# Loading the second phase's weights in two halves, with the turned queries and keys in between

## The reference

```
x = x + self_attention(layernorm(x))     # 16 heads of 128, q and k rms-normed, softmax, wo
x = x + cross_attention(layernorm(x), ctx)  # 16 heads of 32, causal mask; Wq, Wkv_expand, Wout
x = x + ffn(layernorm(x))                # 512 -> 1408 -> 512 (Wg, Wu, Wd), with 8 low-rank
                                         # experts (Ag Bg Au Bu Ad Bd), the top 2 of 8 by router Wr
```

## Time and profile before

| | |
|---|---|
| median of 3 runs | 2593.97 us (2593.64 to 2600.76) |
| the profiled execution, its own time | 2594.01 us |
| its span | 2592.2 us |
| mean granted clock of TensorE | 0.981 of full speed |
| TensorE busy | 2473.8 us |
| DVE, ACT, POOL busy | 1558.7, 1337.1, 870.1 us |
| first phase | from the start to about 1260 us |

### The profile page before, as it was taken

The page is one execution under the profiler, slowest core; times in us unless marked ns, Lnnn a source line. Parts: engine busy times, 40 slices in busy tenths (PEclk is TensorE's granted clock), DMA queues, the critical chain, the costliest instruction groups (busy, mean ns, idle before and its releaser), DMA issues.

```text
span 2592.2 us, 47471 instructions
## 1 busy us (share of the span) xinstructions
PE 2473.8 (95%) x16414; PEld 1335.5 (52%) x16414; DVE 1558.7 (60%) x3578; ACT 1337.1 (52%) x4095; POOL 870.1 (34%) x801
## 2 busy tenths in 40 slices
PE   6999999999999999999889999999999999999988
PEld 3544455554554555445454464464464464465466
DVE  6777756666666666667456655555655645645634
ACT  4555555555555555555445554454454454554433
POOL 2333333333333333333123323323323323423412
PEclk9999999999999999999969999999999999999999
DMA  5677677876786767796511001001001001000000
GB/s 155 149 179 173 142 158 153 180 164 155 156 175 143 171 144 187 161 201 151 137 48 33 32 2 36 16 2 37 15 3 37 9 10 37 3 16 25 7 17 8
DMA packets 455391, 235.24 MB, mean 91 GB/s; under 512 B 389096, under 2 KB 391784, under 8 KB 455144
## 3 DMA queue, kind: packets, MB, share of 16 engines
q1 hardware_dynamic: 455144, 232.08, 38.6%
HBM read 78.66 MB, written 32.77 MB: 43 GB/s over the span
## 4 chain that ended last, share of the span: by engine, by line
PE 84%; DVE 6%; issue 4%; ACT 2%; POOL 1%; DMA 1%; SPq 1%; DVEq 0%; POOLq 0%; ACTq 0%
PE ps L1509 22%; PE ps L1510 22%; PE ps L1511 22%; PE ps L1682 3%; PE ps L1683 2%; PE ps L1684 2%; PE ps L1796 2%; PE ps L1780 1%; PE ps L1692 1%; PE ps L1696 1%; PE ps L1694 1%; PE ps L1616 1%; PE ps L1752 1%; PE ps L1774 1%; ACT mem L955 1%
## 5 line engine op out<-in xcount | busy, mean ns | idle before, releaser
L1509 PE MATMUL ps<-mem 128*128 128x512 f16 (+7 forms) x3932 | 1206.3, 326 | 67.0 <-issue 22.2
L1510 PE MATMUL ps<-mem 128*128 128x512 f16 (+7 forms) x3932 | 1219.6, 325 | 0.0
L1511 PE MATMUL ps<-mem 128*128 128x512 f16 (+7 forms) x3932 | 1202.8, 325 | 0.0
L1509 PEld LDWEIGHTS ps<-mem 128*128 128x128 f16 (+3 forms) x3932 | 407.7, 104 | 390.4 <-issue 65.3
L1511 PEld LDWEIGHTS ps<-mem 128*128 128x128 f16 (+3 forms) x3932 | 409.1, 104 | 312.3 <-issue 11.0
L1510 PEld LDWEIGHTS ps<-mem 128*128 128x128 f16 (+3 forms) x3932 | 410.6, 104 | 299.3 <-issue 10.4
L741 POOL TENSOR_TENSOR mem<-mem 128x500 f32<-128x500 f32 (+1 forms) x231 | 271.4, 1175 | 358.8 <-ACT mem L1031 166.1
L691 POOL TENSOR_TENSOR mem<-mem 128x8 f32<-128x8 f32 x100 | 163.7, 1637 | 516.9 <-DVE mem L1105 516.9
L835 ACT ACTIVATE mem<-ps,mem 100x100 f32<-100x100 f32 x512 | 169.2, 345 | 223.9 <-DVE mem L1135 222.9
L1463 DVE TENSOR_TENSOR mem<-mem 128x500 f16<-128x500 f32 (+1 forms) x231 | 144.2, 648 | 185.8 <-ACT mem L1013 181.7
L703 POOL TENSOR_TENSOR mem<-mem 100x400 f16<-100x400 f32 x128 | 158.8, 1241 | 175.8 <-ACT mem L845 175.8
(11 more groups left out here) (124 smaller groups left out, 3174.3 us busy)
## 6 DMA issues: line engine op xcount, KB each, us to landing
x<-mem SPq DMA_DIRECT2D x100, 256.0 KB, 2.8
mem<-x SPq DMA_DIRECT2D x75, 256.0 KB, 3.6
mem<-in_x SPq DMA_DIRECT2D x50, 256.0 KB, 3.5
mem<-x SPq DMA_DIRECT2D x12, 1000.0 KB
mem<-mem SPq DMA_DIRECT2D x32, 200.0 KB
out<-mem SPq DMA_DIRECT2D x6, 1000.0 KB
mem<-in_wq SPq DMA_DIRECT2D x16, 256.0 KB, 4.0
mem<-in_wk SPq DMA_DIRECT2D x16, 256.0 KB, 4.3
```

Of the source, the lines that this page charges most:

```text
L1509: pe.matmul(out_ap, ah, bh, start=(i == 0), stop=False)
L1510: pe.matmul(out_ap, ah, bl, start=False, stop=False)
L1511: mm = pe.matmul(out_ap, al, bh, start=False, stop=(i == len(pairs) - 1))
```

## The change

Each load of a piece is made as two DMAs. A piece of several chunks is halved by chunks, a piece of one chunk by columns. In the loop the first half is issued where the whole piece was, the second half at the end of the step's work on SP, behind `turn_probs` and `turn_tile`. ACT waits for both halves before it splits (32 instead of 16 counts of the semaphore). The three pieces behind the loop are loaded as two halves one right after the other.

```diff
+            def load_half_b(n, second):
+
+                src, chunks, width, _ = B_PIECES[n]
+                if before_b(n) >= 0 and not second:
+                    sp.wait_ge(c["wlo"], before_b(n) + 1)
+                to = stage_b[:, slot_b(n), 0:chunks * width].rearrange("p (c n) -> p c n", c=chunks)
+                if chunks > 1:
+                    a, b = ((0, chunks // 2), (chunks // 2, chunks))[second]
+                    sp.dma_start(to[:, a:b, :], src[:, a:b, :]
+                                 ).then_inc(c[f"wld{slot_b(n)}"], 16)
+                else:
+                    a, b = ((0, width // 2), (width // 2, width))[second]
+                    sp.dma_start(to[:, :, a:b], src[:, :, a:b] if len(src.shape) == 3 else src[:, a:b]
+                                 ).then_inc(c[f"wld{slot_b(n)}"], 16)
+
             def load_piece_b(n):
-
-                src, chunks, width, _ = B_PIECES[n]
-                if before_b(n) >= 0:
-                    sp.wait_ge(c["wlo"], before_b(n) + 1)
-                sp.dma_start(stage_b[:, slot_b(n), 0:chunks * width].rearrange(
-                    "p (c n) -> p c n", c=chunks), src).then_inc(c[f"wld{slot_b(n)}"], 16)
+                load_half_b(n, False)
+                load_half_b(n, True)
@@ for n in range(FIRST_STEP, STEPS + 3):
-                    load_piece_b(k)
+                    load_half_b(k, False)
...
                 for u in projected_at(n - 1):
                     turn_tile(u)
+                for k in b_pieces_loaded(n):
+                    load_half_b(k, True)
@@ def split_b_hi(n):
-                act.wait_ge(c[f"wld{slot_b(n)}"], 16 * fills_b(n))
+                act.wait_ge(c[f"wld{slot_b(n)}"], 32 * fills_b(n))
```

## The result

The changed kernel takes 2608.28 us (median of 8 runs, 2602.47 to 2614.87), the kernel before 2594.98 in its 8 runs (2592.24 to 2600.76): 13.3 us more, a ratio of 1.0054 with a 95% interval of 1.0043 to 1.0066. It is slower, as forecast (2606.2 us). Of all the executions reported here one, at 3122.55 us and a granted clock of 0.777, was in a slow state of the chip and is left out of every median and ratio.

What follows compares the result with a forecast made beforehand. TensorE was taken as the bound, busy 2473.8 of 2592.2 us. Stalls less gain, 0.5 + 3.9 + 4.5 + 2.7 + 0.8 - 0.2 = 12.2 us, gave 2606.2 us (forecast 2602 to 2610; range 2597.5 to 2615).

Steps and rivals of the forecast that it cites:

- all is the same and shifted: Sign for the changed profile past 1300 us: no change there except a shift in time.
- Piece 1: Cwo's second half, issued behind tile 80's turn: ACT stalls 3.9 us (3.0 to 5.9), TensorE loses 3.9 us.
- Piece 7: wg's first chunk, in the step loading second-phase keys: ACT stalls some 10 us, slack 5.4; 4.5 us lost (2 to 8).
- Piece 11: wu's first chunk, behind tile 99's turn: ACT stalls 3.6 us, slack 0.9, loss 2.7 us (1.9 to 4.8).
- Pieces 0 and 12: Steps without a tile's turn, on a chain without slack: 0.5 and 0.8 us lost, from 0 to about 2 each.
- The hidden pieces: Pieces 2, 4, 5, 6, 8 and 10: second halves land after ACT's old start, but slack hides them, costing nothing.
- The gain of 0.2: Turns behind half a piece land sooner; only those of tiles 91 and 99 gate TensorE; 0.2 us gained.
- Rival (b): SP's turns are the true gate and land 1 to 2 us sooner: 9.6 us of gaps vanish, 2584.4 us; chance 0.07.

## Why the prediction was right, point by point

- **The direction and the sum.** 12.2 us were forecast and 13.3 measured. Removing the move (0.9998) and splitting it between two kernels (1.0051 and 1.0009) show that the move is the cause and that pieces 1, 7 and 11 hold nearly all of it, as the prediction said. That the sum came so close is in part luck. It was a sum of idle time; of that the stretch shows 10.7 us, made up of other parts. The clock, which the sum left out, adds about 5, and some 3 came back in the second phase, where the prediction had "all is the same and shifted".
- **Piece 1: 3.9 us.** ACT waited 4.50 us, and TensorE's gap grew by 5.1, from 0.57 to 5.65. Undersized by 1.2 us of idle: about half of this is the landing, 4.5 us and not 3.8; the rest, 0.6 us by which the gap grew more than ACT's wait, stays open. The halved clock behind it, 3.0 us more, was no term of the sum.
- **Piece 7: 4.5 us.** ACT's wait of 9.90 us was forecast as some 10. The slack behind it was forecast as 5.4; in the six kernels with this half late and no products added in step 113 ACT's wait less TensorE's gap is 4.3 to 5.1 us, so the mechanism held: a held turn makes the half late, and the slack is taken off. The size was too large. The gaps of 4.84 and 0.44 us stand in place of 1.35, 0.71 and 1.87, only 1.4 us more: score products 116, which wait for tile 91 and which the prediction had some 5 us late, waited 0.44. With 2.1 us of clock that is 3.5. (The 3.7 between score products 107 and 116 also hold 1.8 us of new gaps behind piece 6, less the 1.7 that the clock had cost there before.) And the cause of the held turn was wrong: the prediction put it to the keys. Moving them left ACT's wait where it was, and spreading the rows' load freed the turn's issue. The prediction had not looked at line 517.
- **Piece 11: 2.7 us.** ACT waited 3.54 us, TensorE 2.78. Right in size.
- **Pieces 0 and 12: 0.5 and 0.8.** ACT waited 1.41 and 1.84 us, 0.9 and 0.3 more than before. The end of the stretch cost 4.2 us with piece 11's 2.8; the gap at 1269.52 is 1.9 us shorter than in the earlier trace rows, and 3.4 us more at the lower clock fell there. Not resolved further.
- **The hidden pieces at nothing.** Nearly: the kernel with only the others and pieces 0 and 12 late is 2.3 us over the kernel before, with an interval that just reaches none. Two new gaps of 1.17 and 0.64 us behind piece 6 are part of it.
- **The gain of 0.2.** "Issue" did not fall, tile 99's gap stayed (1.42 us, 1.41 before), and a turned tile landed in 4.7 us (median) after, 4.8 before: half a piece less ahead of them did not bring the turns sooner. Rival (b) rested on that.
- **Readings.** The prediction gives the value products one wait of 0.57 us for DVE line 1150; the view has two, 2.1 us in all. Of the 8.2 us of "issue" it names 4.0 and leaves out the largest gap, 2.62 us at 1062.69, and 1.29 at 1208.44. Its issue time of 0.43 to 0.57 us per piece holds for all pieces but two, which took 1.13 and 1.45 (cwo and ad).
- **What it left out.** The granted clock. The windows give it 3.4 us net over the first two places (3.0 and 2.1, less the 1.7 of before). Filling the gaps removed the halved clock and did not shorten the kernel, so what it is worth in the end stays open; so does why the gap for piece 7 is 4.8 us in the changed kernel and 7.9 in two others with the same order in step 111 (2.9 in the one with the rows split). ACT's waits there were 9.9, 13.0 and 12.5 us (7.9), so it lies in when the half lands and not on TensorE.

The rule that the prediction cites from the Trainium skill ("DMA: Bandwidth & Descriptors", "Anatomy of one DMA"), about 2.0 us plus the bytes at 436 GB/s, is given there for DMAs that GpSimd issues; the prediction does not say so, and all DMAs of this kernel are issued by SP. For a half of 352 KB it makes 2.8 us, an estimate. The second halves of this size took 3.3 to 4.8 us in the changed kernel, and 8.5 in one other. The measurement decides: behind turns the halves land 0.5 to 2 us later than by the rule, and in step 111 much later.

## What to carry to other kernels

Before moving a load behind other entries of its queue, compare two times from the trace: when the last of those entries is issued, plus a landing, and when the consumer began before. If the consumer had not waited, the difference is a stall on its engine, and the slack from there to the bounding engine says what is paid. Take the landing times of the entries ahead from the trace as well, not only their issue: in step 111 the half landed just behind the turn, however early it was issued. Look at every step by itself: three of thirteen places held nearly all of the loss, and the others waited 15 us on ACT for at most 5. When a small entry of a queue takes long to issue, read the DMA engines' share at that time: a steady 5 of 16 pointed to a load on 125 partitions, and making it 112 and 13 was worth 5 us (0.10 to 0.29%) in the kernel before, without any move.

## What the runs showed of the hardware that I had not expected

- Behind a load of 1000 KB onto 125 partitions the DMA engines stood at 0.32 to 0.33 for 6 us, and the transposing DMA behind it took 8.5 and 9.3 us to issue (keys moved away). As 112 and 13 partitions the same turn took 2.35 us, and with the keys in place 4.36, with the engines at 0.98 and 337 GB/s from 1120 to 1122 us.
- A half piece on SP's queue behind that turn landed 1.0 to 3.1 us after the turn in seven kernels, 4.8 to 8.5 us after its own issue.
- With a gap of TensorE of 4.8 to 5.7 us in a dense stretch the granted clock was at half for 6.8 us in the changed kernel, and with the gap filled it stayed full. The gap before score products 107, 2.4 to 2.8 us in every trace, was followed by 3.4 us at half in some of them (2.62 us, kernel before) and by none in others (2.83 us, changed kernel).
- Added products in the gaps kept the clock up behind them and bought no time: the lead went to later gaps (1.0071 and 1.0045, against 1.0054 for the changed kernel).
